# Decoder of two blocks, second cross attention: the mask of one quarter of the heads added by a bf16 pass on TensorE

## The chip, the cores and the metric

The kernel runs on one core of a Trainium2 chip. The metric is the device time of one execution in microseconds (us), the median of the runs. A profiled execution of the same program gives the page and the trace.

## The reference

Two decoder blocks work on x (32 batch elements of 128 tokens, 128 features) with a context of the same shape. The first has a recurrent token mixer, two attentions and a feed-forward part, and eight experts; the second has self attention, a cross attention and a mixture of eight experts with a capacity. Only the cross attention of the second block matters here:

```python
scores = jnp.einsum('bhqd,bhkd->bhqk', q, k) * SCALE      # 16 heads of 8
scores = jnp.where(mask == 0, NEG_INF, scores)            # mask int32, (32, 1, 128, 128)
attn = jax.nn.silu(scores)                                # no softmax
out = jnp.einsum('bhqk,bhkd->bhqd', attn, v)
```

The projected output is added to x and layer-normalised. Since silu of a very large negative score is 0, a masked place may be made 0 after the silu (a product with 0 or 1) or made very negative before it (a sum with -1e30).

## The kernel before

The program goes through six stages, each ended by a barrier over the engines; the stage of this cross attention is the fifth. Its functions are `attnx_pe`, `attnx_act`, `attnx_dve`, `attnx_pool` and `attnx_sp`, one for each engine's queue, and the order of the work on each engine is written out by hand in a loop over steps. A step t deals with one batch element per kind of work, at different depths of the pipeline; `need` and `wait_ge` wait for counts of semaphores.

- TensorE (`attnx_pe`), step t: weigh(t-1) (L1700: attention times values, 16 small matmuls), project(t+2) (L1672, L1673: values and queries into bank 5, after the queries of t+1 were read from it), turn(t+3) (L1664: transposes of x, context and mask), score(t+1) (L1688: four matmuls, one for each quarter of the heads, each of 32 rows and 512 columns, into banks 0 to 3, which the silus of t must have read), output(t-1) (L1708), key(t+2) (L1679). An f32 matmul shows as two matmul records and two weight loads.
- ScalarE (`attnx_act`): four silus (L1735), one for each bank, which write `lx_w`; then heads (L1741), turned (L1746: the transposed x, context and mask), keys (L1729).
- VectorE (`attnx_dve`): mask(t, 0..3) (L1780: `lx_w` of a quarter times the transposed mask, 128x512 f32 in place), residual(t-1) (L1786, then the statistics L1788 and L1790), values(t+2) (L1767), queries(t+2) (L1772).
- GpSimd (`attnx_pool`): for each four elements it turns the int32 mask into 0 or 1 in f32 (L1811), which `turn` waits for; for each element the inverse deviation (L1819, L1821) and the normalisation that writes x (L1823).
- SyncE (`attnx_sp`): loads the masks of four elements by one transfer (L1829).

The first block's attention adds its key mask on TensorE, by bf16 passes ahead of the scores (L726, then L733), with one pass for each half of the rows.

Of the kernel before, what the change touches and what calls it, by code (L numbers as in the profile page):

```python
# [6 lines left out]
BF16 = mybir.dt.bfloat16  # L7
ALU = mybir.AluOpType
# [3 lines left out]
B, T, D = 32, 128, 128  # L12
NB = 4
# [23 lines left out]
MASKED = -1e30  # L37
# [10 lines left out]
def build(nc, ins, out):  # L48
    ctx = ExitStack()
    with ctx:  # L50
        def sb(name, shape, dt=F32):
            return ctx.enter_context(nc.sbuf_tensor(name, shape, dt))
# [4 lines left out]
        bank = [ctx.enter_context(nc.psum_tensor(f"bank{i}", [128, BANK], F32)) for i in range(8)]  # L57
# [8 lines left out]
        ident = sb("ident", [128, 128])  # L66
# [319 lines left out]
        r = Room()  # L386
# [259 lines left out]
        r = Room()  # L646
# [19 lines left out]
        def need(eng, s, count):  # L666

            if count > 0:
                eng.wait_ge(s, count)
# [314 lines left out]
        r = Room()  # L984
# [356 lines left out]
        r = Room()  # L1341
# [297 lines left out]
        r = Room()  # L1639
        QUADS = 4  # L1640
        lx_xcm = [r.take(3, T) for _ in range(4)]
        lx_mi = [r.take(NB, T).bitcast(mybir.dt.int32) for _ in range(2)]
        lx_mf = [r.take(NB, T) for _ in range(2)]
        lx_q = [r.take(QUADS, T) for _ in range(2)]
        lx_k = [r.take(T) for _ in range(2)]
        lx_v = [r.take(QUADS, D) for _ in range(4)]
# [12 lines left out]
        def attnx_pe(pe):  # L1659
            def turn(b):  # L1660
                pe.wait_ge(lx.mask_f, b // NB + 1)
                need(pe, lx.turned_sb, b)
                for k, src in enumerate((X[:, b, :], C[:, b, :], lx_mf[(b // NB) % 2][:, b % NB, :])):
                    last = nc.tensor.transpose(bank[4][:, k * T:(k + 1) * T], src, ident[:])  # L1664
                last.then_inc(lx.turned, 1)

            def project(b):
                xT, cT = lx_xcm[b % 4][:, 0, :], lx_xcm[b % 4][:, 1, :]
                pe.wait_ge(lx.turned_sb, b + 1)
                need(pe, lx.q_sb, b)  # L1670
                need(pe, lx.v_sb, b)
                nc.tensor.matmul(bank[5][:, 0:D], cT, w_l1x[:, 2, :], start=True, stop=True)  # L1672
                nc.tensor.matmul(bank[5][:, D:D + T], w_l1x[:, 0, :], xT, start=True, stop=True).then_inc(lx.vq, 1)  # L1673

            def key(b):
                pe.wait_ge(lx.turned_sb, b + 1)
                need(pe, lx.heads_sb, b - 2)
                need(pe, lx.k_sb, b)
                nc.tensor.matmul(bank[7][:, T:2 * T], w_l1x[:, 1, :], lx_xcm[b % 4][:, 1, :], start=True, stop=True)\  # L1679
                    .then_inc(lx.k, 1)  # L1680

            def score(b):
                pe.wait_ge(lx.q_sb, b + 1)
                pe.wait_ge(lx.k_sb, b + 1)
                need(pe, lx.silu, QUADS * b)
                for i in range(QUADS):
                    p = 32 * i
                    last = nc.tensor.matmul(bank[i][:, :], lx_k[b % 2][p:p + 32, :],  # L1688
                                            lx_q[b % 2][p:p + 32, :, :].rearrange("p s t -> p (s t)"),
                                            start=True, stop=True)  # L1690
                last.then_inc(lx.scores, 1)

            def weigh(b):
                pe.wait_ge(lx.masked, QUADS * (b + 1))
                pe.wait_ge(lx.v_sb, b + 1)
                need(pe, lx.heads_sb, b)
                need(pe, lx.k_sb, min(b + 3, B))
                for s in range(QUADS):
                    for j in range(QUADS):
                        last = nc.tensor.matmul(bank[7][32 * j:32 * j + 32, 0:T], lx_v[b % 4][:, s, 32 * j:32 * j + 32],  # L1700
                                                lx_w[b % 2][:, j, s, :], start=(s == 0), stop=(s == QUADS - 1),
                                                skip_group_check=True)
                last.then_inc(lx.pv, 1)

            def output(b):
                pe.wait_ge(lx.heads_sb, b + 1)
                need(pe, lx.res_sum, b)
                nc.tensor.matmul(bank[6][:, 0:D], lx_headsT, w_l1x[:, 3, :], start=True, stop=True)\  # L1708
                    .then_inc(lx.out_ready, 1)

            for t in range(-3, B + 1):
                if t >= 1:
                    weigh(t - 1)
                if 0 <= t + 2 < B:
                    project(t + 2)
                if t + 3 < B:
                    turn(t + 3)
                if 0 <= t + 1 < B:
                    score(t + 1)
                if t >= 1:  # L1720
                    output(t - 1)
                if 0 <= t + 2 < B:
                    key(t + 2)

        def attnx_act(act):
            def keys(b):
                act.wait_ge(lx.k, b + 1)
                need(act, lx.scores, b - 1)
                nc.scalar.activation(lx_k[b % 2], bank[7][:, T:2 * T], ACT.Identity, bias=cols["l1x_bk"][:, 0:1])\  # L1729
                    .then_inc(lx.k_sb, 1)  # L1730

            def silu(b, i):
                act.wait_ge(lx.scores, b + 1)
                need(act, lx.pv, b - 1)
                nc.scalar.activation(lx_w[b % 2][:, i, :, :].rearrange("p s t -> p (s t)"), bank[i][:, :], ACT.Silu,  # L1735
                                     scale=DH1 ** -0.5).then_inc(lx.silu, 1)

            def heads(b):
                act.wait_ge(lx.pv, b + 1)
                need(act, lx.out_ready, b)  # L1740
                nc.scalar.activation(lx_headsT, bank[7][:, 0:T], ACT.Copy).then_inc(lx.heads_sb, 1)  # L1741

            def turned(b):
                act.wait_ge(lx.turned, b + 1)
                need(act, lx.masked, QUADS * (b - 3))
                nc.scalar.activation(lx_xcm[b % 4].rearrange("p k t -> p (k t)"), bank[4][:, 0:3 * T], ACT.Copy)\  # L1746
                    .then_inc(lx.turned_sb, 1)

            for t in range(-3, B + 1):
                now = 0 <= t < B  # L1750
                if now:
                    for i in range(QUADS):
                        silu(t, i)
                if t >= 1:
                    heads(t - 1)
                if t + 3 < B:
                    turned(t + 3)
                if 0 <= t + 2 < B:
                    keys(t + 2)

        def attnx_dve(dve):
# [15 lines left out]
            def mask(b, i):  # L1777
                dve.wait_ge(lx.silu, QUADS * b + i + 1)
                w = lx_w[b % 2][:, i, :, :]
                nc.vector.tensor_tensor(w, w, lx_xcm[b % 4][:, 2, :].unsqueeze(1).to_broadcast([128, QUADS, T]),  # L1780
                                        ALU.mult).then_inc(lx.masked, 1)
# [14 lines left out]
            for t in range(-2, B + 1):  # L1796
                now = 0 <= t < B
                if now:
                    for i in range(QUADS):
                        mask(t, i)  # L1800
                if t >= 1:
                    residual(t - 1)
                if 0 <= t + 2 < B:
                    values(t + 2)
                    queries(t + 2)

        def attnx_pool(pool):
            def mask(n):
                pool.wait_ge((lx.mask_in_even, lx.mask_in_odd)[n % 2], 16 * (n // 2 + 1))
                need(pool, lx.turned, NB * (n - 1))  # L1810
                nc.gpsimd.tensor_scalar(lx_mf[n % 2], lx_mi[n % 2], 0, 0, ALU.is_equal, ALU.is_equal)                    .then_inc(lx.mask_f, 1)  # L1811

            mask(0)
            mask(1)
            for b in range(B):
                if b % NB == 2 and b // NB + 2 < NIT:
                    mask(b // NB + 2)
                pool.wait_ge(lx.stats, b + 1)
                nc.gpsimd.tensor_tensor(lx_var, lx_mv[b % 2][:, 1:2], lneps[:, 0:1], ALU.add)  # L1819
                pool.drain()  # L1820
                nc.gpsimd.tensor_tensor(lx_rstd[b % 2], lx_var, half[:, 0:1], ALU.pow)  # L1821
                pool.drain()  # L1822
                nc.gpsimd.tensor_scalar(X[:, b, :], lx_res[b % 2], lx_mv[b % 2][:, 0:1], lx_rstd[b % 2][:, 0:1],  # L1823
                                        ALU.subtract, ALU.mult).then_inc(lx.normed, 1)
# [9 lines left out]
        r = Room()  # L1834
# [626 lines left out]
```

## Time and profile before

| | |
|---|---|
| median of 3 runs | 2141.43 us (2139.82 to 2145.59) |
| profiled execution, its own time | 2141.83 us |
| its span, first to last instruction | 2140.1 us |
| busy over the span | PE 89%, PEld 70%, DVE 67%, ACT 55%, POOL 23% |
| mean granted TensorE clock | 0.949 |
| chain that ended last | issue 66%, POOL 14%, PE 10%, POOLq 8%, DVE 1%, DMA 1% |

PE is TensorE's matmuls, PEld its weight loads, DVE VectorE, ACT ScalarE, POOL GpSimd. The busy shares are averages over all stages. In the views a time is given from the span's start; "<-" in brackets names what ended an engine's idle time, and "issue" is idle time for which the profile shows no wait. Ends of matmuls are modelled. A row that merges several instructions gives their joint time.

### The profile page before, as it was taken

To read this page: it belongs to the slowest core of one execution; us is meant where nothing else is said; L and a number is where in the kernel's file an instruction comes from. 1 tells how busy PE (TensorE), PEld (TensorE's weight loads), DVE (VectorE), ACT (ScalarE), POOL (GpSimd) and SP (SyncE) were. 2 spreads that over 40 slices of the span, in tenths; PEclk is the share of its full clock that TensorE was granted. 3 is DMA by queue.
4 is the path that set the end of the run, shared out by engine and by line. 5 is a ranking of instruction groups with operands and counts; after the bars stand their busy time and mean duration, and the time that the engine had idled before them with its cause. 6 is when DMAs were issued, how large, how long until landed. Compare 5 with 4: busy or idle time off the path is not lost.

```text
span 2140.1 us, 47673 instructions
## 1 busy us (share of the span) xinstructions
PE 1910.4 (89%) x16935; PEld 1495.1 (70%) x16935; DVE 1433.9 (67%) x3525; ACT 1184.3 (55%) x3926; POOL 500.2 (23%) x812
## 2 busy tenths in 40 slices
PE   3548999999999999999869999978888688699998
PEld 1227888888888888888647777756666455467776
DVE  4775777777777777777556757568888599444443
ACT  2215666666677776666524444447777466133333
POOL 2101111111111111111122212024444477111110
PEclk9668999999999999999879999989999899599999
DMA  7000000000000000000100000010000000000000
GB/s 213 28 0 2 2 2 2 2 2 2 2 2 2 2 2 2 2 2 2 59 12 1 1 1 1 1 35 2 2 2 2 26 17 2 1 0 11 6 6 20
DMA packets 29438, 25.64 MB, mean 12 GB/s; under 512 B 5260, under 2 KB 25748, under 8 KB 29208
## 3 DMA queue, kind: packets, MB, share of 16 engines
q1 hardware_dynamic: 29208, 22.62, 3.6%
q8 instruction: 138, 2.26, 0.4%
q14 instruction: 92, 0.75, 0.1%
HBM read 20.52 MB, written 2.10 MB: 11 GB/s over the span
## 4 chain that ended last, share of the span: by engine, by line
issue 66%; POOL 14%; PE 10%; POOLq 8%; DVE 1%; DMA 1%; DVEq 0%; ACT 0%; SPq 0%
POOL X L1823 3%; POOL work L946 2%; PE bank L1944 2%; PE bank L1931 2%; PE bank L1933 2%; POOL work L1614 2%; POOLq L949 1%; POOL H L950 1%; POOL work L934 1%; POOL work L1039 1%; POOL X L1624 1%; PE bank L1911 1%; POOLq L1613 1%; POOLq L1822 1%; POOLq L1623 1%
## 5 line engine op out<-in xcount | busy, mean ns | idle before, releaser
L814 ACT ACTIVATE work<-bank,work 128x128 f32<-128x128 f32 x1024 | 364.6, 405 | 223.8 <-DVE work L867 223.8
L694 PE MATMUL bank<-work,wbig 128*128 128x128 f32 x2048 | 261.9, 276 | 0.6 <-ACT work L855 0.5
L814 ACT ACTIVATION_READ_ACCUMULATOR work<-bank,work 128x1 f32 x1024 | 250.2, 244 | 0.0
L694 PEld LDWEIGHTS bank<-work,wbig 128*128 128x128 f32 x2048 | 245.6, 193 | 1.2 <-ACT work L855 0.8
L874 DVE TENSOR_TENSOR work<-work 128x512 f32<-128x512 f32 x256 | 177.3, 693 | 24.4 <-issue 6.4
L867 DVE TENSOR_REDUCE work<-bank 128x4 f32<-128x512 f32 x256 | 159.0, 684 | 33.7 <-PE bank L733 33.7
L829 ACT ACTIVATE work<-bank 128x512 f32<-128x512 f32 x256 | 170.5, 667 | 13.2 <-PE bank L707 13.2
L707 PE MATMUL bank<-ident,work 128*128 128x128 f32 x1024 | 156.4, 275 | 3.1 <-DVE work L874 3.1
L2104 DVE TENSOR_TENSOR work<-wff,bank 128x320 f32<-128x320 f32 (+1 forms) x128 | 62.5, 489 | 128.2 <-ACT wff L2019 127.7
L707 PEld LDWEIGHTS bank<-ident,work 128*128 128x128 f32 x1024 | 119.1, 141 | 40.4 <-issue 19.0
L1173 ACT ACTIVATE work<-bank,col_b 128x512 f32<-128x512 f32 x128 | 87.2, 687 | 106.8 <-PE bank L1101 106.6
L1479 ACT ACTIVATE work<-bank,work 128x128 f32<-128x128 f32 x512 | 141.7, 433 | 1.2 <-DVE work L1511 1.2
L944 POOL TENSOR_TENSOR work<-work,lneps 128x1 f32<-128x1 f32 x64 | 12.2, 191 | 550.4 <-DVE work L914 550.4
L1109 PEld LDWEIGHTS bank<-wff,work 128*128 128x128 f32 x1024 | 123.3, 192 | 24.4 <-issue 24.4
L700 PE MATMUL bank<-wbig,work 128*128 128x512 f32 x256 | 137.4, 619 | 0.8 <-ACT work L823 0.8
L733 PEld LDWEIGHTS bank<-work 64*128 64x128 f32 x2048 | 135.0, 188 | 4.0
L887 DVE COPY work<-bank 128x512 f32<-128x512 f32 x128 | 88.6, 692 | 72.1 <-PE bank L700 72.1
L733 PE MATMUL bank<-work 64*128 64x128 f32 x2048 | 135.0, 272 | 0.0
L823 ACT ACTIVATE work<-bank 128x512 f32<-128x512 f32 x192 | 131.3, 684 | 4.7 <-PE bank L694 4.7
L752 PE MATMUL bank<-wbig,work 128*128 128x128 f32 x1024 | 131.3, 281 | 0.9 <-DVE work L862 0.9
L717 PE MATMUL bank<-work 128*64 128x128 f32 x2048 | 127.6, 278 | 0.0
L717 PEld LDWEIGHTS bank<-work 128*64 128x64 f32 x2048 | 112.0, 138 | 21.1 <-issue 20.3
(283 smaller groups left out, 4005.1 us busy)
## 6 DMA issues: line engine op xcount, KB each, us to landing
wbig<-in_moe_w SPq DMA_DIRECT2D x2, 1536.0 KB, 9.3
work<-in_mask_l SPq DMA_DIRECT2D x8, 256.0 KB, 2.8
out<-X SPq DMA_DIRECT2D x8, 256.0 KB, 2.3
H<-in_moe_w SPq DMA_DIRECT2D x3, 512.0 KB, 5.8
wff<-in_moe_w SPq DMA_DIRECT2D x1, 1024.0 KB
wbig<-in_sa_wq SPq DMA_DIRECT2D x1, 512.0 KB, 3.8
wbig<-in_sa_wk SPq DMA_DIRECT2D x1, 512.0 KB, 4.5
wbig<-in_sa_wv SPq DMA_DIRECT2D x1, 512.0 KB, 6.5
```

What stands on the lines that cost most here:

```text
L694: last = nc.tensor.matmul(o[:, j * T:(j + 1) * T], w[:, t * 128:(t + 1) * 128], src, start=True, stop=True)
L700: nc.tensor.matmul(ring(step, place)[:], cT, wv[:, j * 512:(j + 1) * 512], start=True, stop=True)\
L707: last = nc.tensor.transpose(o[:, h * T:(h + 1) * T], at_probs[:, g, h, :], ident[:])
L717: last = nc.tensor.matmul(o[odd * DH0:(odd + 1) * DH0, t * T:(t + 1) * T], at_v[u % 2][:, head * DH0:(head + 1) * DH0], at_probsT[:, 2 * h ...
L733: last = nc.tensor.matmul(bank[2 * pair + odd][:, h * T:(h + 1) * T], at_q[u % 2][p:p + DH0, t, :], at_k[u % 2][p:p + DH0, t, :], start=Fa ...
L752: last = nc.tensor.matmul(ring(step, place)[:, 0:D], at_headsT[:, t, :], wo[:, t * D:(t + 1) * D], start=(t == 0), stop=(t == NT0 - 1))
L814: last = nc.scalar.activation(at_probs[:, g, h, :], bank[g][:, h * T:(h + 1) * T], ACT.Exp, bias=at_nmax[:, g, h:h + 1], accum_out=at_den[ ...
L823: nc.scalar.activation(dst.rearrange("p t n -> p (t n)"), ring(step, place)[:, :], ACT.Copy, scale=DH0 ** -0.5 if piece < 2 else 1.0).then ...
L829: nc.scalar.activation(at_probsT[:, g, :, :].rearrange("p h t -> p (h t)"), ring(step, place)[:, :], ACT.Copy).then_inc(at.probsT_sb, 1)
L867: nc.vector.tensor_reduce(at_nmax[:, g, :], bank[g][:, :].rearrange("p (h t) -> p h t", h=GH), AX.X, ALU.max, negate=True).then_inc(at.max ...
L874: nc.vector.tensor_tensor(at_probs[:, g, :, :], at_probs[:, g, :, :], at_recip[:, g, :].unsqueeze(2).to_broadcast([128, GH, T]), ALU.mult)\
L1479: last = nc.scalar.activation(l1_probs[b % 2][:, g, h, :], bank[g][:, h * T:(h + 1) * T], ACT.Exp, bias=l1_nmax[b % 2][:, g, h:h + 1])
```

## The change

Before the four score matmuls of an element, TensorE writes one bank (bank 3, the quarter `TIMES` = 3) with a bf16 matmul: the mask of the element, scaled to -1e30 where it is 0 and 0 elsewhere, as stationary operand (`lx_mb`), and the identity four times side by side as moving operand. It waits for the silus of the element before, as the scores did. The fourth score matmul then adds to this bank. VectorE multiplies only three quarters; the weighing waits for three products and for the silus. GpSimd makes `lx_mb` from the int32 mask in one more pass per four elements, ahead of the f32 one, and copies the identity to bf16 once.

```diff
         lx_mf = [r.take(NB, T) for _ in range(2)]
+        lx_mb = [r.take(NB * T // 2).bitcast(BF16).rearrange("p (b t) -> p b t", b=NB) for _ in range(2)]
+        lx_ident = r.take(T // 2).bitcast(BF16)
+        TIMES = QUADS - 1
...
             def score(b):
+                need(pe, lx.silu, QUADS * b)
+                nc.tensor.matmul(bank[TIMES][:, :].rearrange("p (s t) -> p s t", s=QUADS), lx_mb[(b // NB) % 2][:, b % NB, :],
+                                 lx_ident.unsqueeze(1).to_broadcast([128, QUADS, T]),
+                                 start=True, stop=False, skip_group_check=True)
                 pe.wait_ge(lx.q_sb, b + 1)
                 pe.wait_ge(lx.k_sb, b + 1)
-                need(pe, lx.silu, QUADS * b)
                 for i in range(QUADS):
                     p = 32 * i
                     last = nc.tensor.matmul(bank[i][:, :], lx_k[b % 2][p:p + 32, :],
                                             lx_q[b % 2][p:p + 32, :, :].rearrange("p s t -> p (s t)"),
-                                            start=True, stop=True)
+                                            start=(i < TIMES), stop=True, skip_group_check=True)
...
             def weigh(b):
-                pe.wait_ge(lx.masked, QUADS * (b + 1))
+                pe.wait_ge(lx.masked, TIMES * (b + 1))
+                pe.wait_ge(lx.silu, QUADS * (b + 1))
...
             def turned(b):
-                need(act, lx.masked, QUADS * (b - 3))
+                need(act, lx.masked, TIMES * (b - 3))
...
                 if now:
-                    for i in range(QUADS):
+                    for i in range(TIMES):
                         mask(t, i)
...
             def mask(n):
                 pool.wait_ge((lx.mask_in_even, lx.mask_in_odd)[n % 2], 16 * (n // 2 + 1))
-                need(pool, lx.turned, NB * (n - 1))
+                need(pool, lx.scores, NB * (n - 1))
+                nc.gpsimd.tensor_scalar(lx_mb[n % 2], lx_mi[n % 2], 0, MASKED, ALU.is_equal, ALU.mult)
                 nc.gpsimd.tensor_scalar(lx_mf[n % 2], lx_mi[n % 2], 0, 0, ALU.is_equal, ALU.is_equal)                    .then_inc(lx.mask_f, 1)

+            nc.gpsimd.tensor_copy(lx_ident, ident[:, :])
             mask(0)
             mask(1)
```

## Rows read from the trace of the kernel before

**Rows 1.** Windows of the stage: length, busy time of each engine, clock, DMA.
```profile
core 0: us, PE busy (x) PEld busy (x) DVE busy (x) ACT busy (x) POOL busy (x), PEclk, DMA share, GB/s
...
1730.00:1748.00 18.00, 15.46 (x213) 10.16 (x217) 16.68 (x38) 12.15 (x30) 13.14 (x13) 1.00 0.06 17
```

**Rows 2.** Timeline of VectorE, two steps: start, time, engine, line, operation.
```profile
1739.86 2.49 DVE L1780 TENSOR_TENSOR work<-work 128x512 f32<-128x512 f32 x4
1742.58 0.29 DVE L1786 TENSOR_TENSOR work<-bank,X 128x128 f32<-128x128 f32 x1 [0.23 <-PE bank L1708]
...
1743.64 0.74 DVE L1772 SCALAR_TENSOR_TENSOR work<-bank,col_l1x_bq,work 128x512 f32<-128x512 f32 x1
1744.30 2.58 DVE L1780 TENSOR_TENSOR work<-work 128x512 f32<-128x512 f32 x4
1747.02 0.29 DVE L1786 TENSOR_TENSOR work<-bank,X 128x128 f32<-128x128 f32 x1
```

**Rows 3.** Timeline of TensorE's matmuls, the same step.
```profile
1744.48 0.46 PE L1672 MATMUL bank<-wsmall,work 128*128 128x128 f32 x2
...
1745.11 0.27 PE L1664 MATMUL bank<-ident,C 128*128 128x128 f32 x1
1745.22 0.27 PE L1664 MATMUL bank<-ident,work 128*128 128x128 f32 x1
1745.42 1.14 PE L1688 MATMUL bank<-work 32*128 32x512 f32 x8
1746.49 0.49 PE L1708 MATMUL bank<-wsmall,work 128*128 128x128 f32 x2
```

**Rows 4.** Timeline of TensorE near the stage's end, without turns.
```profile
1816.29 1.14 PE L1688 MATMUL bank<-work 32*128 32x512 f32 x8
...
1820.57 1.14 PE L1688 MATMUL bank<-work 32*128 32x512 f32 x8 [0.87 <-ACT work L1735]
```

**Rows 5.** Timeline of TensorE in the first block's attention.
```profile
709.27 0.39 PE L726 MATMUL bank<-keymask,onerow 64*128 64x512 bf16 x2
709.50 1.05 PE L733 MATMUL bank<-work 64*128 64x128 f32 x16
710.39 0.38 PE L726 MATMUL bank<-keymask,onerow 64*128 64x512 bf16 x2
710.60 1.05 PE L733 MATMUL bank<-work 64*128 64x128 f32 x16
```

**Rows 6.** Timeline of TensorE's weight loads, the step of rows 3.
```profile
1744.45 0.30 PEld L1672 LDWEIGHTS bank<-wsmall,work 128*128 128x128 f32 x2 [0.33 <-issue]
...
1745.42 0.31 PEld L1688 LDWEIGHTS bank<-work 32*128 32x128 f32 x8 [0.17 <-issue]
```

**Rows 7.** Windows at the start of the stage and behind its end.
```profile
1678.00:1681.00 3.00, 2.85 (x13) 2.00 (x16) 1.19 (x3) 1.21 (x3) 0.00 (x0) 0.50 0.20 59
...
1834.00:1838.00 4.00, 4.00 (x21) 4.00 (x21) 0.69 (x1) 0.00 (x1) 0.00 (x0) 0.50 0.00 0
```

**Rows 8.** Timeline of ScalarE, the step of rows 3.
```profile
1743.07 2.05 ACT L1735 ACTIVATE work<-bank 128x512 f32<-128x512 f32 x4
```

**Rows 9.** Timeline of the stage's start.
```profile
1672.43 3.83 POOL L1811 TENSOR_SCALAR work<-work 128x512 f32<-128x512 int32 x2 [3.21 <-DMA work<-in_mask_l]
...
1674.52 0.45 PE L1664 MATMUL bank<-ident,X 128*128 128x128 f32 x1 [8.22 <-POOL work L1811]
```

**Rows 10.** Timeline of GpSimd, and its line L1624 (stage before) as a group.
```profile
1735.79 2.02 POOL L1823 TENSOR_SCALAR X<-work 128x128 f32<-128x128 f32 x1 [0.17 <-issue]
1737.79 2.01 POOL L1811 TENSOR_SCALAR work<-work 128x512 f32<-128x512 int32 x1
...
1805.75 0.19 POOL L1819 TENSOR_TENSOR work<-work,lneps 128x1 f32<-128x1 f32 x1 [1.35 <-DVE work L1790]
...
L1624 POOL TENSOR_SCALAR X<-work 128x128 f32<-128x128 f32 x32 | 25.6, 802 | 5.6 <-issue 5.6
```

**Rows 11.** Timeline of the stage's end.
```profile
1823.02 2.46 DVE L1780 TENSOR_TENSOR work<-work 128x512 f32<-128x512 f32 x4
...
1825.54 0.81 PEld L1700 LDWEIGHTS bank<-work 128*32 128x32 f32 x32 [1.18 <-DVE work L1780]
```

## The prediction

> **What bounds the kernel now.** The stretches first [rows 1]: the stage runs from about 1672 to 1830 us, and in its steady part VectorE is the busiest engine, 16.68 of 18 us, before TensorE with 15.46 at full clock. That makes taking a quarter of the mask products from VectorE look like a gain. A busy share does not say which wait ends last, so I went on to the timelines of one step (one batch element). The chain that ended last is no help here: in this stage it runs through GpSimd, an engine that waits for the statistics in most steps.
>
> The period. The residual add (L1786) starts at 1742.58 and again at 1747.02 [rows 2]: 4.44 us a step. What starts each one? In the first of these steps the four products took 2.49 us and ended at 1742.35; in the second they took 2.58 and ended at 1746.88. The 0.09 us that the first step won was lost again in front of the residual (idle 0.23, released by TensorE), and the period stayed. So the products are not what the residual waits for. The output projection L1708 is: it starts at 1746.49 and is over, by its modelled end, at 1746.98 [rows 3], 0.04 before the residual.
>
> This closes **a cycle that has no product in it**. On VectorE: residual 1742.58, statistics, values, queries until 1744.38 [rows 2], 1.80 us. The projection of the next element reuses the bank that the queries read, and starts 0.10 later at 1744.48. On TensorE in program order: projection, three turns, scores at 1745.42, output until 1746.98 [rows 3], 2.50 us. Then 0.04 to the residual. 1.80 + 0.10 + 2.50 + 0.04 = 4.44, the whole period.
>
> Two loops lie just below it. VectorE by itself: from the residual's start 1.72 to the first product, 2.58 for four, and the residual could follow at once: 4.30, or 4.24 if it overlaps the last product as neighbours there do. ScalarE with TensorE: scores to the end of the key projection, keys, four silus, and then the next scores, which overwrite the banks that the silus read. At the end of the stage, where no turns are left, this loop shows itself: scores at 1816.29 and 1820.57 [rows 4], 4.28 a step.
>
> **The change part by part.**
>
> Removed: the fourth product, 2.58 / 4 = 0.645 us of VectorE a step. It lies beside the cycle of 4.44, so it saves nothing in the steady part; VectorE's loop falls to 4.24 - 0.645 = 3.6 and idles more.
>
> Added on TensorE: for each of 32 elements a weight load (128x128, bf16) and a matmul of 512 columns in bf16, between the turns and the scores. That is inside the 2.50 us leg of the cycle, and also inside the silu loop. The trace has the same kind of pass in the first block: a bf16 mask pair, one pass on each half of the rows, starts at 709.27 and 710.39, and the f32 scores behind it at 709.50 and 710.60 [rows 5]: 0.23 and 0.21 us of delay. I take 0.22. Its weight load (0.10 for a pair) hides behind the turns, as loads of one tile shape do. The scores use another shape: they start 0.20 after the last turn, where turns follow each other at 0.11 [rows 3], and their load starts together with them [rows 6]. That 0.09 exists now and moves behind the pass, unless its cause is the scores' three waits, two of which would then be settled during the pass; in that case a step pays 0.22 - 0.09 = 0.13. That is the lower bound. It could go below if the pass streamed behind the turns, but nothing here starts a second full-array matmul before the first has streamed: not free. Upper bound: the whole record of a pass, 0.38 [rows 5], if bf16 behind f32 drained the array. I take 0.22, since [rows 5] have this very pass ahead of f32 scores. 32 x 0.22 = +7.0. The first pass falls into half clock [rows 7] and takes twice as long: +0.2.
>
> The silu wait that now stands before the pass: the silus end at 1745.12 [rows 8] and the last turn starts at 1745.22, so it was already met before the turns ended; the longer step makes it looser. The added silu wait in the weighing (L1700) is met too: the weighing starts only after the next keys, which ScalarE runs behind all four silus and more. Queued behind it are projection and turns, unaffected.
>
> Check of the loops with the pass in: cycle 4.66, silu loop 4.28 + 0.22 = 4.50, VectorE 3.6. TensorE alone now leaves its loads idle for 0.33 before the projection [rows 6], so 4.11 + 0.22 = 4.33. The cycle stays the bound, the step becomes 4.66.
>
> Added on GpSimd: a copy of the identity (128x128), before the first mask; GpSimd waits for the mask's transfer until 1672.43 anyway [rows 9], so it costs nothing (without that cover about a quarter of the 1.92 of a pass with four times its columns, 0.5). And a second pass over each mask of four elements, ahead of the one that releases the turns. The first two took 3.83, so 1.92 each [rows 9]. At the start of the stage TensorE stands idle for it (8.22 released by L1811), nothing covers it: +1.9. Between half and double that is the bound, as its bf16 output is not in the trace. Six later ones (b = 2, 6, ... 22) cost nothing: GpSimd has some 1.3 us spare in each step [rows 10], is late by about 2 at most, and its results are due almost two steps after the statistics. The mask pair for four elements is due over a step later. SyncE's mask loads are released 2 us later and have three steps of room.
>
> At the end of the stage the last element's products do stand on the path: the last weighing waits 1.18 us for VectorE [rows 11]. Three instead of four of 2.46 / 4: -0.6.
>
> **Sum.** 2141.83 (span 2140.1 plus 1.7 around it) + 7.0 + 0.2 + 1.9 - 0.6 = 2150.3. The median of the runs, 2141.43, is 0.4 lower: **2150 us**, +0.40%. A difference under 0.3%, 6.4 us, can't be told from none.
>
> **Rivals.**
>
> The cheap pass. The step pays 0.13 instead of 0.22: 32 x 0.13 = 4.2, with 1.5 for the ends: 2147.1, within 0.3%. For it: the gap of [rows 6]. Against it: the same gap stands where tile shapes change, and two or three met waits ahead of other loads cost nothing. The Trainium skill (TensorE: Matmul & The Clock Gate, Back-to-back issue gap) gives about 131 ns as sustained spacing of matmuls of 512 columns and 216 ns for an isolated one; with the first, 32 passes would be an estimated 4.2 us, the same result. By that page's second figure the trace agrees (0.21 to 0.23).
>
> VectorE is the bound after all, the other side. If the products end the wait before the residual and the pass vanishes in TensorE's gap, the step falls to the silu loop, 4.28: 28 steps x 0.16 = -4.5, +1.9 - 0.6: 2138. It decides only if the pass costs under 0.1 and the residual follows the products. Against it: the won 0.09 us that changed nothing [rows 2]. If only its first half held, the silu loop with the pass (4.50) would still be above 4.44.
>
> The dear pass: 0.38 a step, 12.2 + 1.5: 2155.
>
> The port. GpSimd's normalisation takes 2.02 beside the products, and 0.80 for the same form in the stage before [rows 10]: the two engines disturb each other. GpSimd's mask pass of 2.01 us ended at 1739.80, just before the products began at 1739.86 [rows 2, 10]; a second one would run on into them. If it held the first product back for its 2.0 us, VectorE's slack (4.66 - 1.72 - 1.94 = 1.0) would be exceeded by 1.0 six times: 2156. Against it: beside GpSimd's 2.02 the products lose 0.09, so GpSimd is the one that yields. The Trainium skill (SBUF — State Buffer, SBUF: two separate sides) calls the shared port an exclusive lock that goes to whoever starts first, which speaks for this rival; a full block of VectorE is in no row here.
>
> That the change isn't what it says: VectorE's loop runs over three quarters and the count it signals is waited for in threes; I see no way for a fourth product.
>
> A last uncertainty is TensorE's clock: full in the steady part, half at the start of the stage [rows 7] and again after its end, where 20 us of dense work run at half speed. Shifted idle times could move these by 1 to 2 us either way.
>
> **How the numbers follow.** Forecast (2150) 0.68, cheap pass 0.17, VectorE bound 0.04, dear pass 0.06, port 0.05. Some 0.04 of the forecast's own spread falls under 2147.9. Slower 0.75, same 0.21, faster 0.04. The range: from the cheap pass less 1.5 for the clock, 2145.5, to the dear pass and the port with theirs, 2156.5.
>
> **What would show it.** Residual to residual 4.66 instead of 4.44; scores 0.41 or so after the last turn instead of 0.20; three products in 1.9 and VectorE idle about 1 us before the residual, released by the output projection; the first turn near 1676.4. Wrong if the step stays under 4.5, if VectorE's idle before the residual doesn't grow, or if a step with a mask on GpSimd is longer than its neighbours.

## The result, and the profile after

The changed kernel takes 2151.06 us (median of 6 runs, 2148.82 to 2152.48), the kernel before 2141.32 (6 runs, 2139.51 to 2145.59). The ratio is 1.0044, with a 95% interval of 1.0031 to 1.0057: slower by 9.7 us, 2150.0 was forecast. The profiled execution took 2151.82 us, its span 2150.1, 10.0 longer than before. Of the runs further below one execution, of the kernel with three products, fell into a slower state (3061.64 us at a granted clock of 0.603) and is left out of its ratio.

First the views in which the cost appears. VectorE, two steps of the steady part, to be laid beside [rows 2]:

```profile
1745.17 2.18 DVE L1787 TENSOR_TENSOR work<-work 128x512 f32<-128x512 f32 x3
1748.10 0.29 DVE L1793 TENSOR_TENSOR work<-bank,X 128x128 f32<-128x128 f32 x1 [0.76 <-PE bank L1715]
...
1750.08 1.89 DVE L1787 TENSOR_TENSOR work<-work 128x512 f32<-128x512 f32 x3
1753.02 0.29 DVE L1793 TENSOR_TENSOR work<-bank,X 128x128 f32<-128x128 f32 x1 [1.05 <-PE bank L1715]
```

The residual (now L1793) starts at 1748.10, and in the step of the kernel's usual length that went before it at 1743.45: 4.65 us. Three products take 1.89 alone, and VectorE then stands idle for 1.05 until the output projection (L1715) is done. Before, that idle time was 0.23 or nothing. In the waits of the steady part the same shows in one row each, before (1694 to 1820 us) and after (1702 to 1827 us):

```profile
DVE work L1786 <- PE bank L1708: 1.4, 6, 0.2
```

```profile
DVE work L1793 <- PE bank L1715: 25.6, 26, 1.1
```

(Who waited for whom; then the total in us, the number of waits, the longest.) VectorE waits 26 times for the output instead of 6 times. VectorE's busy time in a window of 18 us fell from 16.68 to 13.26, TensorE's stayed near the 15.46 of [rows 1], spread over a longer step (columns as in [rows 1]):

```profile
1742.00:1760.00 18.00, 15.20 (x204) 9.61 (x205) 13.26 (x32) 11.26 (x27) 13.41 (x15) 1.00 0.06 17
```

TensorE's matmuls in the step that began at 1743.45, to be laid beside [rows 3]:

```profile
1745.35 0.46 PE L1675 MATMUL bank<-wsmall,work 128*128 128x128 f32 x2
...
1745.98 0.27 PE L1667 MATMUL bank<-ident,C 128*128 128x128 f32 x1
1746.09 0.27 PE L1667 MATMUL bank<-ident,work 128*128 128x128 f32 x1
1746.20 0.38 PE L1687 MATMUL bank<-work 128*128 128x512 bf16 x1
1746.51 1.14 PE L1694 MATMUL bank<-work 32*128 32x512 f32 x8
1747.58 0.49 PE L1715 MATMUL bank<-wsmall,work 128*128 128x128 f32 x2
```

The pass (L1687) joins the stream of the turns at 0.11 us, the scores start 0.31 behind it: 0.42 from the last turn to the scores instead of 0.20. From the projection to the output it is now 2.23 (1745.35 to 1747.58), before 2.01. The weight loads show where the change of tile shape sits:

```profile
1746.09 0.10 PEld L1687 LDWEIGHTS bank<-work 128*128 128x128 bf16 x1
1746.50 0.31 PEld L1694 LDWEIGHTS bank<-work 32*128 32x128 f32 x8 [0.32 <-issue]
```

The pass's own load of 0.10 lies behind the turns. The load of the scores starts only together with their matmul, as in [rows 6]: the 0.09 that the trace shows at a change of tile shape (0.20 instead of 0.11) has moved behind the pass, it was not filled.

Where the 10.0 us of span went, read from the two timelines (the end points are starts of the named instructions):

| stretch | before | after | difference |
|---|---|---|---|
| up to the stage's first mask transfer | 1669.38 | 1670.02 | +0.6 |
| from there to the first turn | 5.14 | 6.89 | +1.75 |
| first turn to first residual (three passes, and another clock) | 19.00 | 20.03 | +1.0 |
| 27 steady steps, to the last residual behind turns | 120.09 | 126.26 | +6.2 |
| from there to the next stage's first matmul | 16.94 | 16.79 | -0.15 |
| the rest | | | +0.6 |

The steady step is 4.655 against 4.439, so 27 x 0.216 = 5.8 of the 6.2. The remainder is one step more that is a few tenths too long (see the last section). The -0.15 is two steps at 4.51 instead of 4.28, less 0.6 for the missing last product. The +1.0 is the sum of two opposite parts. From the first turn to the second scores the changed kernel is 0.5 quicker, a pass included (11.29 against 11.80), since TensorE came to full clock earlier (its first scores take 1.14 us instead of 1.71). From the second scores to the third it is 1.5 slower (7.08 against 5.61): its second scores run mostly at half clock (1.72 us), those of the kernel before at full clock (1.14), and its third pass at half clock too.

The start and the end of the stage, beside [rows 9] and [rows 11]:

```profile
1670.02 11.14 SPq L1838 DMA_DIRECT2D work<-in_mask_l  x4
...
1670.12 0.29 POOL L1821 CAST work<-ident 128x128 bf16<-128x128 f32 x1 [0.26 <-POOLq L332]
...
1672.84 1.94 POOL L1818 TENSOR_SCALAR work<-work 128x512 bf16<-128x512 int32 x1 [2.44 <-DMA work<-in_mask_l]
1674.85 1.92 POOL L1819 TENSOR_SCALAR work<-work 128x512 f32<-128x512 int32 x1
...
1676.91 0.45 PE L1667 MATMUL bank<-ident,X 128*128 128x128 f32 x1 [9.97 <-POOL work L1819]
...
1682.18 0.38 PE L1687 MATMUL bank<-work 128*128 128x512 bf16 x1
...
1682.49 1.14 PE L1694 MATMUL bank<-work 32*128 32x512 f32 x8
```

```profile
1826.12 1.14 PE L1694 MATMUL bank<-work 32*128 32x512 f32 x8
...
1830.63 1.14 PE L1694 MATMUL bank<-work 32*128 32x512 f32 x8
...
1833.07 1.86 DVE L1787 TENSOR_TENSOR work<-work 128x512 f32<-128x512 f32 x3
...
1834.99 0.81 PEld L1707 LDWEIGHTS bank<-work 128*32 128x32 f32 x32 [0.57 <-DVE work L1787]
```

GpSimd's copy of the identity takes 0.29 while the mask is still on its way. The f32 mask (L1819) stands behind the bf16 one (L1818) and the first turn behind both. At the end the last weighing waits 0.57 for VectorE instead of 1.18.

### The profile page after: what moved, and what is told of

Its sections match the earlier page's. It is cut to its first block, busy times and chain, and to the rows that moved or that the text cites. A ratio compares the mean times of both kernels' runs of the same rounds, so it can differ in the third digit from the quotient of the medians.

```text
span 2150.1 us, 47714 instructions
## 1 busy us (share of the span) xinstructions
PE 1919.2 (89%) x16967; PEld 1499.3 (70%) x16967; DVE 1413.4 (66%) x3493; ACT 1182.3 (55%) x3926; POOL 508.4 (24%) x821
## 4 chain that ended last, share of the span: by engine, by line
issue 66%; POOL 14%; PE 10%; POOLq 8%; DVE 1%; DMA 1%; DVEq 0%; ACT 0%; SPq 0%
POOL X L1832 2%; POOL work L946 2%; PE bank L1953 2%; PE bank L1940 2%; PE bank L1942 2%; POOL work L1614 2%; POOLq L949 1%; POOL H L950 1%; POOL work L934 1%; POOL work L1039 1%; POOL X L1624 1%; PE bank L1920 1%; POOLq L1613 1%; POOLq L1831 1%; POOLq L1623 1%
## 5 line engine op out<-in xcount | busy, mean ns | idle before, releaser
L829 ACT ACTIVATE work<-bank 128x512 f32<-128x512 f32 x256 | 168.1, 658 | 13.4 <-PE bank L707 13.4
L823 ACT ACTIVATE work<-bank 128x512 f32<-128x512 f32 x192 | 129.0, 672 | 4.7 <-PE bank L694 4.7
L752 PEld LDWEIGHTS bank<-wbig,work 128*128 128x128 f32 x1024 | 120.8, 194 | 8.9 <-issue 1.3
```

The lines of the kernel that those rows point to most:

```text
L752: last = nc.tensor.matmul(ring(step, place)[:, 0:D], at_headsT[:, t, :], wo[:, t * D:(t + 1) * D], start=(t == 0), stop=(t == NT0 - 1))
L823: nc.scalar.activation(dst.rearrange("p t n -> p (t n)"), ring(step, place)[:, :], ACT.Copy, scale=DH0 ** -0.5 if piece < 2 else 1.0).then ...
L829: nc.scalar.activation(at_probsT[:, g, :, :].rearrange("p h t -> p (h t)"), ring(step, place)[:, :], ACT.Copy).then_inc(at.probsT_sb, 1)
```

## The experiments

All were timed beside the kernel before on the same chip; "step" is residual to residual in the profiled execution of each.

**The product alone.** VectorE's loop runs over three quarters, nothing replaces the fourth: this kernel leaves a quarter of the heads unmasked. The waits count three products, and the weighing waits for the silus, as in the changed kernel.

```diff
-                    for i in range(QUADS):
+                    for i in range(QUADS - 1):
                         mask(t, i)
```

> The kernel before with the fourth quarter's mask product left out and nothing put in its place (a quarter of the heads is not masked). Theory (the cycle output, residual, statistics, values, queries, projection, turns, scores, output has no product in it): residual to residual stays 4.44 us, the total falls only by the stage's tail, 0.6 us, to about 2140.7. Rival (VectorE's products end the wait before the residual): the step falls at least to the silu loop's 4.28, so the total falls by 4.5 + 0.6 us or more, to 2136 or less.

Measured: ratio 1.0002 (0.9992 to 1.0012), step 4.44.

```profile
1773.80 0.29 DVE L1787 TENSOR_TENSOR work<-bank,X 128x128 f32<-128x128 f32 x1 [0.83 <-PE bank L1709]
...
1775.52 1.89 DVE L1781 TENSOR_TENSOR work<-work 128x512 f32<-128x512 f32 x3
1778.24 0.29 DVE L1787 TENSOR_TENSOR work<-bank,X 128x128 f32<-128x128 f32 x1 [0.84 <-PE bank L1709]
```

VectorE is idle for 0.84 in every step and the step has not changed by a hundredth. The product's time was not on the path, which the 0.09 us in [rows 2] had suggested. The total is within its interval both of no change and of the expected -0.6. The executions whose mean granted clock was 0.949 lie closer together: four of this kernel with a median of 2141.5 (2141.01 to 2141.85), seven of the kernel before with 2142.0 (2140.92 to 2142.45).

**The pass alone.** The changed kernel with all four products (`for i in range(QUADS)`, counts of `masked` as before).

> The changed kernel with all four products kept, so the bf16 pass and GpSimd's second mask pass alone are added. Theory: the step is 4.655 as in the changed kernel, since VectorE's own loop (4.24 to 4.30) still lies under it; the total is that of the changed kernel plus the tail, 0.6: about 2151.7. Rival (the product's removal did save something): clearly more than that, up to 0.645 a step, 2165 or so.

Measured: 2151.62 us, ratio 1.0037 (1.0022 to 1.0051), step 4.655. The pass and GpSimd's additions make the whole slowdown, and keeping the product costs nothing in the step.

**A fifth product.** A product of the same size into a scratch tile, behind the four.

```diff
+                    nc.vector.tensor_tensor(lx_extra[t % 2], lx_zero,
+                                            lx_xcm[t % 4][:, 2, :].unsqueeze(1).to_broadcast([128, QUADS, T]), ALU.mult)\
+                        .then_inc(lx.masked, 1)
```

> The kernel before with a fifth product of the same size on VectorE in each step (into a scratch tile, its result unused). Theory: VectorE's own loop, 4.24 to 4.30, grows by 0.645 to about 4.89 to 4.94 and becomes the bound: a step 0.45 to 0.50 longer, 13 to 15 us in all, about 2155. Rival (VectorE bounds already at 4.44): 0.645 a step, 5.08, 20 us in all, 2161.

Measured: 2159.68 us, ratio 1.0072 (1.0054 to 1.0090), step 4.81, and 5.22 in most of the steps in which GpSimd makes a mask. The theory's sign and order hold, its size for VectorE's loop does not: 4.81 less one product (0.64) is 4.17, under the 4.24 to 4.30 I had taken. The total, above the expected 2155, comes in part from something that the expectation left out (five steps of 5.22 make 2 us; one of 6.38, on which see the last section, another 1.6):

```profile
1721.66 0.68 DVE L1804 TENSOR_TENSOR work<-work 128x512 f32<-128x512 f32 x1
...
1722.26 0.28 DVE L1788 TENSOR_TENSOR work<-bank,X 128x128 f32<-128x128 f32 x1
...
1726.34 2.02 POOL L1817 TENSOR_SCALAR work<-work 128x512 f32<-128x512 int32 x1
...
1726.47 1.09 DVE L1804 TENSOR_TENSOR work<-work 128x512 f32<-128x512 f32 x1
...
1727.48 0.28 DVE L1788 TENSOR_TENSOR work<-bank,X 128x128 f32<-128x128 f32 x1
```

The fifth product (L1804) takes 0.68 in an ordinary step and 1.09 when GpSimd's mask pass (L1817) started 0.13 before it. That is what the port rival spoke of, for 0.41 of the 2.02 us that GpSimd's instruction lasts; that a port is the cause is not shown. It costs time here because VectorE has no slack. In the changed kernel the same happens and is hidden:

```profile
1763.87 1.92 POOL L1819 TENSOR_SCALAR work<-work 128x512 f32<-128x512 int32 x1
1764.05 2.18 DVE L1787 TENSOR_TENSOR work<-work 128x512 f32<-128x512 f32 x3
...
1766.98 0.29 DVE L1793 TENSOR_TENSOR work<-bank,X 128x128 f32<-128x128 f32 x1 [0.76 <-PE bank L1715]
```

Three products take 2.18 instead of 1.89, the idle time shrinks from 1.05 to 0.76, and the step stays 4.65. The Trainium skill (SBUF — State Buffer, SBUF: two separate sides) says the engine that comes second blocks fully until the first is done. The traces agree that VectorE can be held back when GpSimd came first, and not that it lasts: 0.3 to 0.4 us is lost, not what is left of the 2. Nor is it always held. In the kernel with both orders opened and four products (below) the products start 0.97 behind GpSimd's mask pass and take the 2.46 that they take there without it:

```profile
1750.05 1.94 POOL L1811 TENSOR_SCALAR work<-work 128x512 f32<-128x512 int32 x1
...
1751.02 2.46 DVE L1780 TENSOR_TENSOR work<-work 128x512 f32<-128x512 f32 x4
```

**Two passes.** The bf16 matmul issued twice.

> The changed kernel with the bf16 pass issued twice (the second overwrites what the first wrote). Theory: the pass is paid in full on the cycle, and the second costs what a matmul of 512 bf16 columns streams, 0.21 to 0.22 a step: step 4.87, total 7 us more, about 2158. Rival (part of the first pass's cost is a change between f32 and bf16 or a drain, paid once): the second pass costs clearly less than 0.2, the step stays under 4.8.

Measured: 2159.20 us, ratio 1.0071 (1.0054 to 1.0088), step 4.87.

```profile
1755.24 0.27 PE L1667 MATMUL bank<-ident,work 128*128 128x128 f32 x1
1755.35 0.38 PE L1687 MATMUL bank<-work 128*128 128x512 bf16 x1
1755.57 0.38 PE L1690 MATMUL bank<-work 128*128 128x512 bf16 x1
1755.87 1.14 PE L1697 MATMUL bank<-work 32*128 32x512 f32 x8
```

Pass to pass is 0.22, and the second one to the scores 0.30 again. So 0.216 a step is the price of each pass of 512 bf16 columns, and nothing of it is a change of data type paid once.

**The order of the two masks on GpSimd.** The f32 pass first; a semaphore of its own for the bf16 mask.

```diff
-                nc.gpsimd.tensor_scalar(lx_mb[n % 2], lx_mi[n % 2], 0, MASKED, ALU.is_equal, ALU.mult)
                 nc.gpsimd.tensor_scalar(lx_mf[n % 2], lx_mi[n % 2], 0, 0, ALU.is_equal, ALU.is_equal).then_inc(lx.mask_f, 1)
+                nc.gpsimd.tensor_scalar(lx_mb[n % 2], lx_mi[n % 2], 0, MASKED, ALU.is_equal, ALU.mult).then_inc(lx.mask_b, 1)
```

> The changed kernel with GpSimd's f32 mask pass, which the turns wait for, ahead of the bf16 one; the bf16 pass on TensorE waits for the bf16 mask by a semaphore of its own. Theory: the first turn starts one GpSimd pass earlier, about 2.0 us sooner after the mask's transfer, and nothing else moves: about 2149.1. Rival (the startup is set by something else, or TensorE's clock gives the gain back): unchanged within 0.5 us; if the first bf16 pass then waits for its mask, part of the gain only.

Measured: 2148.32 us, ratio 1.0026 (1.0017 to 1.0036).

```profile
1669.68 11.17 SPq L1840 DMA_DIRECT2D work<-in_mask_l  x4
...
1674.59 0.45 PE L1668 MATMUL bank<-ident,X 128*128 128x128 f32 x1 [7.98 <-POOL work L1820]
```

From the transfer to the first turn it is 4.91 instead of 6.89, the expected 2.0. But first turn to first residual also fell, from 20.03 to 18.29, and that is TensorE's clock. The windows from 1690 to 1694 (granted clock third from the end), the changed kernel and then this one:

```profile
1690.00:1694.00 4.00, 3.45 (x38) 2.80 (x39) 1.90 (x3) 2.59 (x6) 0.00 (x0) 0.50 0.02 4
```

```profile
1690.00:1694.00 4.00, 3.45 (x41) 2.15 (x40) 2.25 (x8) 2.39 (x7) 0.10 (x1) 1.00 0.00 0
```

The changed kernel runs there at half clock (1.2 GHz), this one at full (2.4 GHz). The kernel before shows 0.79 in the same window. Ahead of the second scores TensorE had stood idle for some 3.1 us in all three. What decides whether the clock falls I can't read from these traces. It moved the stage by 1.7 us here, so the total gained more than the expected 2.0 (2149.1 was expected): by the ratios to the kernel before, some 3.9.

**The cycle cut on VectorE, in both kernels.** Values and queries ahead of the residual.

```diff
-                if t >= 1:
-                    residual(t - 1)
                 if 0 <= t + 2 < B:
                     values(t + 2)
                     queries(t + 2)
+                if t >= 1:
+                    residual(t - 1)
```

> The kernel before with values and queries ahead of the residual on VectorE. Theory: this cuts the cycle, since the queries no longer stand behind the output; the next bound is the silu loop, 4.28, or VectorE's own, 4.24 to 4.30: step about 4.28 to 4.30, total 4 us less, about 2137. Rival (the period is TensorE's or VectorE's own work): step 4.44 as before.

> The changed kernel with values and queries ahead of the residual on VectorE. Theory: the cycle is cut, the silu loop with the pass bounds: 4.28 + 0.22 = 4.50, as in the changed kernel's last two steps; total about 4.5 us less than the changed kernel, 2146.5. So even with the cycle cut the pass keeps costing, while the saved product pays nothing. Rival: with VectorE off the path the changed kernel gains more than the kernel before does, and comes to its time or under it.

Measured: 2141.46 us for the kernel before so changed, ratio 0.9989 (0.9980 to 0.9999), step 4.32; 2144.03 for the changed one, ratio 1.0006 (0.9996 to 1.0015), step 4.53. The step was set by that cycle: moving three instructions of VectorE shortens it in both kernels by 0.12. Once it is cut the pass costs 0.21 again, as in the cycle. In the first of the two the clock stayed low longer at the start of the stage (first turn to first residual 21.56 instead of 19.00), which ate most of the 3.2 us from 27 steps. That execution had a mean granted clock of 0.946; the two of this kernel with 0.949 took 2137.30 and 2139.09, near the 2137 expected.

The total of the second came out under the expected 2146.5, at the time of the kernel before, which is what its rival named. The steps don't bear the rival out, as they shortened alike in both. The span of its profiled execution is 8.2 under the changed kernel's, and only 3.9 of that lie in the 27 steps. Another 1.5 arose ahead of the stage and 2.9 behind it, where nothing was edited. At the start of the next stage TensorE still had 0.81 of its clock from 1836 to 1840 in this run, and 0.50 from 1840 to 1844 in the changed kernel, whose stage begins 5.3 later.

The next bound is not quite the one I named. In the second kernel:

```profile
1750.63 1.08 PE L1707 MATMUL bank<-work 128*32 128x128 f32 x32 [0.55 <-ACT work L1736]
1751.64 0.49 PE L1675 MATMUL bank<-wsmall,work 128*128 128x128 f32 x2
...
1755.16 1.08 PE L1707 MATMUL bank<-work 128*32 128x128 f32 x32 [0.55 <-ACT work L1736]
```

Weighing to projection is 1.01 without any wait, in the changed kernel 1.17 (1744.18 to 1745.35). I had read 0.33 of idle weight loads before the projection as TensorE's slack; only 0.16 of it was, the rest stands there without a wait. So TensorE's loop through the keys, weighing to weighing, is 4.53 with the pass and 4.31 without (read from the first of the two runs), not 4.33 and 4.11.

**The pass elsewhere.** Into bank 0, which the first silu sets free, ahead of the projection; VectorE leaves out the first product.

```diff
                 if t >= 1:
                     weigh(t - 1)
+                if 0 <= t + 1 < B:
+                    preset(t + 1)          # the bf16 pass, into bank 0
                 if 0 <= t + 2 < B:
                     project(t + 2)
```

> The changed kernel with the pass for bank 0 instead of bank 3 and issued before the projection, where TensorE's loads stand idle for 0.33 waiting for the queries; it then needs only the first silu of the element before. VectorE leaves out the first product instead of the fourth. Theory: in the steady part the pass lies beside the cycle, which is 4.44 to 4.50 again; with GpSimd's pass at the start (+2.0) and the tail (-0.6) the total is 2143 to 2145. Rival (the pass costs its 0.22 wherever it stands): step 4.655, total as the changed kernel.

Measured: 2142.99 us, ratio 1.0002 (0.9992 to 1.0011), step 4.44.

```profile
1753.09 1.08 PE L1711 MATMUL bank<-work 128*32 128x128 f32 x32 [0.55 <-ACT work L1742]
1754.11 0.39 PE L1688 MATMUL bank<-work 128*128 128x512 bf16 x1
1754.33 0.39 PE L1675 MATMUL bank<-wsmall,work 128*128 128x128 f32 x2
...
1755.20 1.14 PE L1698 MATMUL bank<-work 32*128 32x512 f32 x8
```

The pass starts 1.02 behind the weighing, where TensorE would have waited for the queries, instead of 2.02 behind it, and the scores still come in time. The same instruction that cost 5.8 us over 27 steps costs nothing 1.0 us earlier in the step.

**Both orders opened.** Queries first as above, and TensorE in the order projection, turns, (pass), weighing, scores, key projection, output; once with four products and no pass, once with the pass in bank 0, three products and the f32 mask first on GpSimd, once with three products and no pass, which leaves a quarter of the heads unmasked.

```diff
-                if t >= 1:
-                    weigh(t - 1)
                 if 0 <= t + 2 < B:
                     project(t + 2)
                 if t + 3 < B:
                     turn(t + 3)
+                if t >= 1:
+                    weigh(t - 1)
                 if 0 <= t + 1 < B:
                     score(t + 1)
-                if t >= 1:
-                    output(t - 1)
                 if 0 <= t + 2 < B:
                     key(t + 2)
+                if t >= 1:
+                    output(t - 1)
```

> The kernel before (four products, no pass) with both other loops opened: values and queries ahead of the residual on VectorE, and TensorE in the order projection, turns, weighing, scores, key projection, output. Theory: TensorE's loop through the keys (4.31, as the run with queries first alone showed) falls to about 3.8 and the silu loop to about 4.06, so VectorE's own four-product loop, 4.32, is now the bound alone: step 4.32, about 3 us under the kernel before. Every fourth step, in which GpSimd makes a mask, may be up to 0.4 longer, because VectorE has no slack. Rival (there never was a VectorE loop near 4.3 and the queries-first run was bound by TensorE): step 4.1 or less.

> The same reordering with the pass and three products: the pass goes into bank 0, after the turns and ahead of the weighing, so it needs only the first silu of the element before; GpSimd's f32 mask goes ahead of the bf16 one at the start. Theory: VectorE's loop is 3.7, TensorE's about 4.0 with the pass, the silu loop about 4.06 and the bound: step 4.05 to 4.15, 8 to 11 us under the kernel before, about 2132 to 2135, and 6 us or so under its twin with four products. So the same removed product pays 0.2 to 0.25 a step once VectorE is what ends the step. Rival (the pass costs its 0.22 wherever it stands and the product never pays): not faster than its twin.

> The reordered kernel of before (step 4.08, VectorE 95.7 of 100 us busy) with three products instead of four and no pass; a quarter of the heads is not masked. Theory: in that order VectorE's own work is the bound, so this time the removed product does shorten the step, down to the next loop: the reordered kernel with pass and three products stands at 4.06 with TensorE 96.3 of 100 us busy, and the pass takes 0.2 of it, so about 3.85; total 6 us or so under the reordered one, 2125. Rival (the four-product step of 4.08 is already set by TensorE or the silu loop): step 4.06 to 4.08, total within 1 us of it. The difference between this run and the one with the pass is the price of the pass in an order where TensorE is the bound.

Measured: 2131.21 us, ratio 0.9942 (0.9928 to 0.9956), step 4.08; 2131.83, ratio 0.9942 (0.9928 to 0.9955), two steps in four of 4.06, and 4.24 and 4.16 at GpSimd's masks; 2128.83, ratio 0.9943 (0.9925 to 0.9960), step 4.06. The windows from 1700 to 1800 of the three, in this order:

```profile
1700.00:1800.00 100.00, 91.12 (x1234) 60.05 (x1235) 95.69 (x223) 72.85 (x172) 72.23 (x79) 1.00 0.05 13
```

```profile
1700.00:1800.00 100.00, 96.30 (x1258) 61.32 (x1251) 87.08 (x195) 71.67 (x169) 75.82 (x85) 1.00 0.04 13
```

```profile
1700.00:1800.00 100.00, 88.10 (x1243) 59.02 (x1240) 83.77 (x197) 70.40 (x173) 61.99 (x79) 1.00 0.04 13
```

Three expectations fell. Four products fit into 4.08, so VectorE's loop is no more than that in this order, and most of GpSimd's masks lengthen no step there. The kernel with the pass is not some 6 us faster than its twin with four products, but level with it. And taking a product away brings 0.02, not 0.23, because the silu loop stands at 4.06, the size predicted for it. The third kernel's scores wait for the silus:

```profile
1761.54 1.14 PE L1688 MATMUL bank<-work 32*128 32x512 f32 x8 [0.58 <-ACT work L1736]
...
1765.60 1.14 PE L1688 MATMUL bank<-work 32*128 32x512 f32 x8 [0.49 <-ACT work L1736]
```

So in this order two loops lie within 0.02, VectorE with four products (4.08) and the silu loop (4.06), and TensorE, 96% busy with the pass in it, has little left. The pass costs no time in a step without a mask on GpSimd and brings none. Around GpSimd's two mask passes (1700.85 to 1704.85) the second kernel's products are held up again, 2.31 instead of 1.89:

```profile
1702.37 2.31 DVE L1794 TENSOR_TENSOR work<-work 128x512 f32<-128x512 f32 x3 [0.22 <-ACT work L1749]
```

VectorE has little slack for it here, and two steps in four grow by 0.10 and 0.18: 1.7 us over the stage, counted against the third kernel, which the ratios can't resolve. Both full reorderings, with the pass or without it, are 0.6% faster than the kernel before, and so faster than the changed one too.

## Why the prediction was right

**The cycle.** In the prediction its four pieces added up to 4.44 with no product in it. The run with three products (4.44) and the one with queries first (4.32) show both halves of that: the product is not on it, the queries behind the residual are.

**The pass.** 0.22 a step was taken from the bf16 pair in the first block; 0.216 was measured, 4.655 for a forecast of 4.66. The cheap pass (0.13) fell: the 0.09 at the change of tile shape is not made by the scores' waits for semaphores that the pass would cover, since it stands unchanged behind the pass. The dear pass fell with 0.216. The Trainium skill's figure for sustained spacing, 131 ns (TensorE: Matmul & The Clock Gate, Back-to-back issue gap), is not seen here: pass to pass is 0.22, by its figure for an isolated one.

**The start.** +1.9 was forecast, +1.75 measured to the first turn (one more pass of 2.0, the transfer some 0.25 quicker); the order of the masks gives it back in full. First turn to first residual grew by 1.0 where the sum had 0.86 for the passes (three at 0.22 and the 0.2 for half clock). That the two lie close is luck. The first pass ran at full clock (0.31 to the scores) and the third at half (0.56), and on the work around them, which the change did not touch, the clock gave time back up to the second scores and took more behind them. Where the clock stands low could not be foreseen, and the run with the f32 mask first shows what it can be worth: 1.7.

**The end.** -0.6 was forecast; the wait for VectorE fell by 0.61.

**What was covered.** GpSimd's six later passes made no step longer in the changed kernel, as forecast. The disturbance that the port rival named is real, but its price is 0.3 to 0.4 us and not 2.0, and VectorE's slack of 1.05 holds it. The argument against it in the prediction, that GpSimd is the one that yields, was wrong: both lose. The identity's copy (0.29) is under the transfer.

**What was wrong and did not matter.** "TensorE alone ... 4.11 + 0.22 = 4.33": it is 4.31 and 4.53. "VectorE by itself ... 4.24": it is 4.17. Neither was in the sum, since both lie under 4.66, but 4.53 is close enough that a cheaper cycle would have run into it.

The sum for the profiled execution was 2150.3, it took 2151.8. Of the 1.5 between them 0.6 arose ahead of this stage, 0.6 behind it, and 0.3 in a longer step.

## What to carry to other kernels

An engine that is 93% busy need not be the bound. Look for two neighbouring steps in which its work took unequal time: if the period did not follow, removing work from it pays nothing. Then close the loop through the program orders of two engines, and check that its pieces add up to the period; what is added inside that loop costs its full time, and a few instructions moved out of it gain more than an instruction removed beside it. Where work must be added to TensorE, ask first where in the step it waits, and which buffer is free by then: the same pass cost 0.216 a step between turns and scores, and nothing ahead of the projection.

## What the runs showed of the hardware

A product on VectorE with two SBUF operands takes 0.68 us, and 1.09 if a GpSimd instruction of 2 us has started 0.13 before it. Products that begin 0.97 behind the start of such an instruction lose nothing. GpSimd's normalisation takes 2.02 beside the products and 0.80 alone.

The granted clock differs between executions of one kernel. Of 31 executions of the kernel before on one chip, the 16 with a mean of 0.949 or 0.950 took 2140.55 to 2144.25 us, the 8 with 0.946 took 2144.50 to 2147.40. A difference of a few us between two medians can be this and nothing else; the step length is the safer measure.

Some steps are longer with no wait shown. In the kernel before it is one of 4.70; in the changed kernel one of 4.92 and one of 5.02; the run with three products has 4.70 and 4.81. VectorE is idle for 0.17 or 0.29 before its values or queries (L1774, L1779 in the changed kernel) and the profile calls it issue. In the changed kernel and in the runs with three products, two passes, the f32 mask first and the pass elsewhere they are the 12th and the 22nd step each time. The cause is open; nothing was tried on it.

The step of 6.38 in the run with five products begins with such an idle time of 0.44. TensorE waits 1.05 for the queries behind it, and then its clock is at 0.52 from 1789 to 1792 us. The scores there take 2.09 instead of 1.14, and VectorE waits 1.12 for the output. In all the step is 1.6 us longer than its neighbours.
